# Recommender network on one core: eight features looked up by matmuls, comparisons shared by VectorE and GpSimd, products written from ScalarE's queue

## What is computed

```
e = emb_tables[jnp.arange(F)[None, :], x]            # B=1024, F=32, D=64, V=1000
gram = jnp.einsum('bid,bjd->bij', e, e)
iu, ju = jnp.triu_indices(F, k=1)
cross = gram[:, iu, ju]
h = jnp.concatenate([e.reshape(B, F * D), cross], axis=1)
h = jax.nn.relu(h @ W1 + b1)                          # H1=1024
h = jax.nn.relu(h @ W2 + b2)                          # H2=512
logits = h @ W3 + b3                                  # OUT=1000
return jax.nn.sigmoid(logits)
```

## Time and profile before

| what | value |
|---|---|
| three timed runs | 657.92, 658.48 (median), 665.98 us |
| profiled execution, first to last instruction | 660.4 us, on core 0 |
| PE busy | 456.6 us (69%) |
| DVE, ACT, POOL busy | 291.9, 246.6, 269.1 us |
| mean granted clock of PE | 0.852 of full |
| moved by DMA | 67.60 MB, mean 102 GB/s |

### The profile page before, as it was taken

How to read it: one execution, slowest core, us unless ns; L and a number is a source line. 1 busy time by engine, 2 the same in 40 slices (tenths; PEclk the granted TensorE clock), 3 DMA queues, 4 the chain that set the end, 5 groups by cost and what they waited for, 6 DMA issues and landing times.

```text
span 660.4 us, 8819 instructions
## 1 busy us (share of the span) xinstructions
PE 456.6 (69%) x3344; PEld 434.9 (66%) x3344; DVE 291.9 (44%) x461; ACT 246.6 (37%) x449; POOL 269.1 (41%) x265
## 2 busy tenths in 40 slices
PE   0222137572759876676799899811799999999786
PEld 0012127471749876576699889811799899999786
DVE  6210024150324553253546658610546688846641
ACT  3110023130334342152534666500434776834532
POOL 6777717577540377767100378777000000000000
PEclk9997558585769888768699999955799999999989
DMA  6611101131316211332086424411175305186522
GB/s 195 217 51 26 26 6 23 21 95 52 99 33 251 75 25 22 88 102 71 15 288 187 126 58 116 120 26 26 76 262 177 104 23 164 66 279 188 161 90 63
DMA packets 29145, 67.60 MB, mean 102 GB/s; under 512 B 6418, under 2 KB 12722, under 8 KB 28594
## 3 DMA queue, kind: packets, MB, share of 16 engines
q1 hardware_dynamic: 16834, 54.54, 25.7%
q0 software_dynamic: 8192, 8.40, 6.2%
q10 hardware_dynamic: 4080, 4.10, 2.1%
HBM read 56.63 MB, written 10.39 MB: 101 GB/s over the span
## 4 chain that ended last, share of the span: by engine, by line
PE 51%; another core or an unknown queue 17%; issue 11%; DVE 6%; POOL 5%; ACT 5%; DMA 4%; SPq 0%; ACTq 0%
PE h1p L491 11%; PE h1p L493 10%; PE h1p L492 10%; PE misc L524 8%; POOL emb L255 5%; PE misc L491 3%; PE misc L492 3%; PE misc L493 3%; DVE dg L418 2%; PE misc L513 2%; DVE h1p L435 2%; DMA out_dram<-res 2%; ACT whi L299 1%; ACT z L304 1%
## 5 line engine op out<-in xcount | busy, mean ns | idle before, releaser
L255 POOL DMA_INDIRECT emb<-tables_dram,idx x256 | 267.4, 1045 | 184.9 <-PE misc L513 101.7
L491 PE MATMUL h1p<-xhi,whi 128*128 128x256 f32 x512 | 156.4, 306 | 16.8 <-issue 12.7
L493 PE MATMUL h1p<-xhi,wlo 128*128 128x256 f32 x512 | 151.2, 295 | 12.5 <-issue 12.2
L492 PE MATMUL h1p<-xlo,whi 128*128 128x256 f32 x512 | 151.2, 295 | 8.7 <-issue 8.6
L524 PE MATMUL misc<-z 128*128 128x128 f32 x512 | 78.8, 322 | 89.5 <-ACT dg L315 50.3
L524 PEld LDWEIGHTS misc<-z 128*128 128x128 f32 x512 | 74.2, 233 | 93.7 <-ACT dg L315 51.6
L400 DVE TENSOR_TENSOR wlo<-wraw,whi 128x1024 fp32r<-128x1024 f32 (+1 forms) x80 | 97.2, 1215 | 60.7 <-ACT whi L299 60.2
L491 PEld LDWEIGHTS h1p<-xhi,whi 128*128 128x128 f32 x512 | 104.3, 204 | 18.2 <-issue 13.8
L492 PEld LDWEIGHTS h1p<-xlo,whi 128*128 128x128 f32 x512 | 104.1, 203 | 13.9 <-issue 13.6
L493 PEld LDWEIGHTS h1p<-xhi,wlo 128*128 128x128 f32 x512 | 103.8, 203 | 12.6 <-issue 12.2
L299 ACT CAST whi<-wraw 128x1024 fp32r<-128x1024 f32 (+1 forms) x80 | 84.1, 1052 | 57.6 <-PE h1p L493 34.4
(11 more groups left out here) (39 smaller groups left out, 589.1 us busy)
## 6 DMA issues: line engine op xcount, KB each, us to landing
wraw<-w_dram SPq DMA_DIRECT2D x64, 512.0 KB
wraw<-w_dram SPq DMA_DIRECT2D x16, 500.0 KB
wres<-w_dram SPq DMA_DIRECT2D x8, 512.0 KB, 3.6
emb<-tables_dram,idx POOLq DMA_INDIRECT x256
gram_scratch<-dg SPq DMA_DIRECT2D x4, 1024.0 KB, 3.9
out_dram<-res ACTq DMA_DIRECT2D x16, 250.0 KB
gram_scratch<-dg SPq DMA_DIRECT2D x4, 512.0 KB, 4.8
gc<-gram_scratch SPq DMA_DIRECT2D x16, 128.0 KB, 2.8
```

The lines of the kernel that those rows point to most:

```text
L255: nc.gpsimd.indirect_dma_start(emb[:, k, t, f * D:(f + 1) * D], None, tables, bass.IndirectOffsetOnAxis(ap=idx[:, t, 2 * k + f:2 * k + f + ...
L491: nc.tensor.matmul(dst, whi[:, slot, cols], hi, start=start, stop=False, skip_group_check=True)
L492: nc.tensor.matmul(dst, whi[:, slot, cols], lo, start=False, stop=False, skip_group_check=True)
L493: return nc.tensor.matmul(dst, wlo[:, slot, cols], hi, start=False, stop=stop, skip_group_check=True)
```

## The change

- Features 24 to 31 (pairs 12 to 15, `LOOKS`) are no longer gathered. For each pair and block a new step "look" loads the two tables in full as 125 partitions by 8 entries (`VP`, `VC`), splits them like weights into hi and lo side by side, and PE multiplies them with eight 0/1 matrices of 125x256 for each feature: entry [p, c, sample] is 1 where the id is 8p + c. These come from comparisons of the ids (loaded to all partitions by `load_x`) with a constant. Of the eight comparisons of a half-step, DVE makes c < 6 (first block) or c < 5, GpSimd the others, placed between its gathers by `gathers_before`. Three of these matrices' buffers are there (`HOTS`). PE makes 16 matmuls of 125x128 by 256 columns in a look.
- Features 0 to 23 are gathered: 48 gathers a block, in the order of pairs, for both tiles together, into two buffers of `emb`; the wait for the transposes of two blocks before stands from block 2 on. PE transposes two pairs at a time (`tr`), and ACT and DVE then take 128x512 (hi, lo) and two times 64x256 (`z`) in one go.
- Layer 1 follows the tiles as they come, from the first block on (`schedule`), with layers 2 and 3 of the block before between; everything is written out, without hardware loops. No weights stay resident: every step is loaded, six steps ahead.
- `z` uses 64 partitions for each tile, and the products are 128 matmuls of 64x64 with 64 rows each for a block, in 4 groups; ACT and DVE each take two parts of 32x512 from each group.
- `dg` is written to DRAM once (1 MB, without the second copy of 0.5 MB), from ACT's queue, and read back by four DMAs from ACT's queue (`move`); the outputs are issued by SP, after a wait for the sigmoid.
- b1 is a row of the pair weights against a row of ones. ACT applies relu out of PSUM for both hidden layers; the separate passes of DVE (L435) are gone.
- `weight_lo` subtracts in four quarters of 128x256 where it was one instruction of 128x1024.

```diff
+VP, VC = 125, 8
+HOTS = 3
+LEAD = 24
 QB = NB // 4
-GJ = QB // 4
+GROUPS = QB // 16
 CROSS = 4
...
+def schedule():
...
+    yield ("look", 0, 12)
+    for n in range(BLOCKS):
+        yield ("tr", n, 0)
+        yield from emb(n, 12, 0)
+        yield ("look", n, 13)
+        yield from emb(n, 1)
+        yield from l2(n - 1, 0)
+        yield ("tr", n, 1)
+        yield from emb(n, 13)
+        yield from l2(n - 1, 1)
+        yield ("tr", n, 2)
+        yield from emb(n, 2)
+        yield from l2(n - 1, 2)
+        yield ("look", n, 14)
+        yield from emb(n, 3)
+        yield from l2(n - 1, 3)
+        yield ("tr", n, 3)
+        yield from emb(n, 14)
+        yield from l3(n - 1, 0)
+        yield ("look", n, 15)
+        yield from emb(n, 4)
+        yield ("tr", n, 4)
+        yield from l3(n - 1, 1)
+        yield ("tr", n, 5)
+        yield from emb(n, 15, 5)
+        yield ("gram", n)
+        yield from emb(n, 6, 7, 8)
+        yield ("move", n)
+        yield from l3(n - 1, 2)
+        yield from emb(n, 9)
+        yield from l3(n - 1, 3)
+        yield from emb(n, 10)
+        yield ("pairs", n)
+        yield from emb(n, 11)
+        for k in range(CROSS):
+            yield ("pair", n, k)
+        yield ("h1", n)
+        if n + 1 < BLOCKS:
+            yield ("look", n + 1, 12)
+    for k in range(4):
+        yield from l2(BLOCKS - 1, k)
+    for k in range(4):
+        yield from l3(BLOCKS - 1, k)
...
+def first_on_gpsimd(h):
+    return 6 if h < 2 * LOOKS else 5
...
+def gathers_before(h, c):
+    n, at = divmod(h, 2 * LOOKS)
+    ready = (0, 0, 6, 10, 18, 24, 28, 32)[at] if n == 0 else 4 * GT * n + LEAD - 10 + 6 * at
+    return min(BLOCKS * 4 * GT, max(0, ready - 2 * (VC - 1 - c)))
...
+            def load_x(i):
+                if i >= len(LOOKED):
+                    return
+                _, n, k = LOOKED[i]
+                if i >= 2:
+                    sp.wait_ge(s_hotv, 2 * (i - 1))
+                    sp.wait_ge(s_hotp, 2 * (i - 1))
+                src = bass.AP(tensor=xt.tensor, offset=2 * k * B + n * NB, ap=[[0, VP], [B, 2], [1, NB]])
+                sp.dma_start(xb[0:VP, i % 2, :, :], src).then_inc(s_xb[i % 2], 16)
...
+            for kind, n, *k in ITEMS:
+                if (kind, n, *k) in STEP:
+                    load(STEP[kind, n, k[0]] + LOADS_AHEAD)
+                if kind == "look":
+                    load_x(LOOK[kind, n, k[0]] + 2)
+                if kind == "out":
+                    j = k[0]
+                    sp.wait_ge(s_sig, 4 * n + j + 1)
+                    sp.dma_start(out.rearrange("(s p) b -> p s b", p=OT)[:, 2 * j:2 * j + 2, n * NB:(n + 1) * NB],
+                                 res[:, j % 2, :].rearrange("p (s b) -> p s b", s=2)).then_inc(s_out[j % 2], 16)
...
+            def compare(h, c):
+                i, f = divmod(h, 2)
+                if c == first_on_gpsimd(h):
+                    pool.wait_ge(s_xb[i % 2], 16 * (i // 2 + 1))
+                    if h >= HOTS:
+                        pool.wait_ge(s_used, used_after(*LOOKED[(h - HOTS) // 2]))
+                last = nc.gpsimd.tensor_scalar(hot[0:VP, h % HOTS, c, :], xb[0:VP, i % 2, f, :],
+                                               vals[0:VP, c:c + 1], None, ALU.is_equal)
+                if c == VC - 1:
+                    last.then_inc(s_hotp, 1)
+            comparisons = [(h, c) for h in range(2 * len(LOOKED)) for c in range(first_on_gpsimd(h), VC)]
+            gathers = [(n, k, t, f) for n in range(BLOCKS) for k in range(GT) for t in range(BT) for f in range(2)]
+            made = 0
+            for g, (n, k, t, f) in enumerate(gathers):
+                while made < len(comparisons) and gathers_before(*comparisons[made]) <= g:
+                    compare(*comparisons[made])
+                    made += 1
+                m = k // 2
+                if g == 0:
+                    pool.wait_ge(s_idx, 1)
+                if (n, k, t, f) == (1, 0, 0, 0):
+                    pool.wait_ge(s_idx, 2)
+                if n >= 2 and (k % 2, t, f) == (0, 0, 0):
+                    pool.wait_ge(s_t, GP * (n - 2) + m + 1)
+                nc.gpsimd.indirect_dma_start(
+                    emb[:, n % 2, k, t, f * D:(f + 1) * D], None, tables,
+                    bass.IndirectOffsetOnAxis(ap=idx[:, BT * n + t, 2 * k + f:2 * k + f + 1], axis=0),
+                ).then_inc(s_emb[n % 2][m], 16)
+            for h, c in comparisons[made:]:
+                compare(h, c)
...
+            def looked_up_hi(n, k):
+                act.wait_ge(s_used, used_after("look", n, k))
+                read = bank_of("look", n, k)
+                for f in range(2):
+                    nc.scalar.copy(xhi[D * f:D * (f + 1), k, :], read[0:D, f, :])
+                nc.scalar.copy(xlo[0:D, k, :], read[D:P, 0, :]).then_inc(s_zeven, 1)
+            def gram_copies(n):
+                for g in range(GROUPS):
+                    act.wait_ge(s_gram, GROUPS * n + g + 1)
+                    for c in range(2):
+                        last = nc.scalar.copy(dg_of(g, c), gram_diagonal(g, c))
                     last.then_inc(s_dga, 1)
+                if n > 0:
+                    act.wait_ge(s_gc, 64 * n)
+                act.wait_ge(s_dga, GROUPS * (n + 1))
+                act.wait_ge(s_dgv, GROUPS * (n + 1))
+                act.dma_start(gd, dg[:]).then_inc(s_gdw, 16)
+            def move(n):
+                act.wait_ge(s_gdw, 16 * (n + 1))
+                if n > 0:
+                    act.wait_ge(s_gclo, n)
+                else:
+                    act.wait_ge(s_gcones, 1)
+                for kk in range(4):
+                    src = bass.AP(tensor=gd.tensor, offset=(CROSS * kk + 1) * QB,
+                                  ap=[[(F + 1) * QB, F - 1], [F * F * QB, 4], [1, CROSS * QB]])
+                    act.dma_start(gc[F * kk:F * (kk + 1) - 1, :, :, :].rearrange("i c s q -> i c (s q)"),
+                                  src).then_inc(s_gc, 16)
...
+            def weight_lo(u):
+                if u >= len(STEPS):
                     return
+                w = width(STEPS[u][0])
+                dve.wait_ge(s_whi, u + 1)
+                for i in range(4):
+                    part = slice(w // 4 * i, w // 4 * (i + 1))
+                    if STEPS[u][0] == "look":
+                        part = slice(VC // 2 * i, VC // 2 * (i + 1))
+                        last = nc.vector.tensor_tensor(table_part(u % RING, 1)[:, part, :], table_raw(u)[:, part, :],
+                                                       table_part(u % RING, 0)[:, part, :].bitcast(fp32), ALU.subtract)
+                    else:
+                        last = nc.vector.tensor_tensor(wlo(u % RING)[:, part], wraw[:, u % RAWS, part],
+                                                       whi(u % RING)[:, part].bitcast(fp32), ALU.subtract)
+                last.then_inc(s_wlo, 1)
...
+            def compare(i):
+                if i >= len(LOOKED):
+                    return
+                dve.wait_ge(s_xb[i % 2], 16 * (i // 2 + 1))
+                for f in range(2):
+                    h = 2 * i + f
+                    if h >= HOTS:
+                        dve.wait_ge(s_used, used_after(*LOOKED[(h - HOTS) // 2]))
+                    for c in range(first_on_gpsimd(h)):
+                        last = nc.vector.tensor_scalar(hot[0:VP, h % HOTS, c, :], xb[0:VP, i % 2, f, :],
+                                                       vals[0:VP, c:c + 1], None, ALU.is_equal)
+                    last.then_inc(s_hotv, 1)
...
+            def look_up(n, k, slot):
+                i, a = SLOT["look", n, k], LOOK["look", n, k]
+                slot_free(i, n)
+                for f in range(2):
+                    pe.wait_ge(s_hotv, 2 * a + f + 1)
+                    for c in range(VC):
+                        if c == first_on_gpsimd(2 * a + f):
+                            pe.wait_ge(s_hotp, 2 * a + f + 1)
+                        last = nc.tensor.matmul(misc[:, i % 2, NB * f:NB * (f + 1)],
+                                                wsplit[0:VP, slot, P * (VC * f + c):P * (VC * f + c + 1)],
+                                                hot[0:VP, (2 * a + f) % HOTS, c, :], start=(f, c) == (0, 0),
+                                                stop=c == VC - 1, skip_group_check=True)
+                return last
+            def gram(n):
+                pe.wait_ge(s_zeven, SLOTS * (n + 1))
+                pe.wait_ge(s_zodd, SLOTS * (n + 1))
+                if n > 0:
+                    pe.wait_ge(s_sig, outs_before(("gram", n)))
+                for g in range(GROUPS):
+                    if g >= 2:
+                        pe.wait_ge(s_dga, GROUPS * n + g - 1)
+                        pe.wait_ge(s_dgv, GROUPS * n + g - 1)
+                    for q in range(8):
+                        for h in range(2):
+                            for t in range(BT):
```

(4 more changed lines are left out.)

697 lines of the change are left out of this document (321 added, 376 removed).

## The result

The changed kernel takes 634.82 us (median of 4 runs, 632.97 to 637.81). The kernel before, run beside it, takes 662.23 (657.92 to 669.17); the ratio is 0.9597, 95% interval [0.9526, 0.9667]. The forecast was 546 us, in a range of 498 to 632. The sign is right, the time lies outside the range.

A forecast was written before the change was run, and what follows sets the result against it. Before: PE bounds only block 3, and stalls beside dense gathers cost the others. After: PE and DVE together bound the blocks; 142 + 123 + 123 + 118 and a tail of 40 give 546 us, range 498 to 632.

The forecast's parts named there:

- The sign: Whole kernel: faster than before by more than 2% (below 645 us), given a chance of 0.91.
- the write and the read back: Products through DRAM in each block: about 13 us, hidden behind six steps (17 us); up to 10 us if uncovered.
- Block 0's stall: Block 0, gathers 32 to 58 without comparison: a stall mostly covered by the gathers, 2 us added, block 142 us.
- The stalls of blocks 1 and 2: Blocks 1 and 2, beside gathers: comparisons act as pauses, leaving 5 us of stall in each, from 36 and 46.
- Rival B: Blocks 1 to 3: stalls stay because GpSimd's comparisons are no pause for the code; about 626 us, chance 0.18.
- the missing code: Stalls beside gathers: engine code is not delivered while POOL gathers densely, but arrives in a pause of a microsecond.
- Products: PE's 256 product matmuls in each block: 20 us taken, between 7 (side by side in the array) and 28.6.
- A block's DVE: VectorE's work in each of blocks 1 to 3: 105 us, with 1.70 us for a step's four quarter subtractions.
- GpSimd's comparison: One 256-element comparison on POOL between gathers: 0.8 us taken, within 0.3 to 1.3.
- Rival C: Blocks 1 to 3: VectorE is the bound, stopped by GpSimd's comparisons, 136 us a block; about 603 us, chance 0.12.
- Rival D: POOL sets the pace because its comparisons are dear; slower than before from 3.7 us a comparison, chance 0.04.
- Rival E: Looks wait for late 0/1 matrices, so layer 1 does not follow the tiles; 7 us each gives 658, chance 0.04.

The follow-up runs named there:

- e1: Changed kernel with each 31-row read back of the products cut into reads of 16 and 15 rows: 498.14 us, 0.9964 of before.
- f1: Changed kernel run again without edit, in a set where the kernel before took 498.0 us: 597.86 us, 1.1986 of before.
- e2: Changed kernel with the write and the four 31-row reads of the products issued from SyncE's queue instead of ScalarE's: 575.98 us, 1.1536 of before.
- e3: Kernel before the change, with each 32-row read of the products cut into one of 31 rows and one of 1: 572.06 us, 1.1457 of before.
- first set: The first comparison runs, both kernels without edit: changed kernel 634.8 us, kernel before 662.2 us.
- h2: Kernel before with an unused GpSimd comparison after every second gather and POOL's loop written out, beside before at 664.74 us: 602.36 us, 0.908.
- h1: Changed kernel with reads of 16 and 15 rows, all comparisons on VectorE and whole subtractions, beside before at 664.74 us: 626.37 us, 0.9433.
- f2: Kernel before the change, run again without edit for a trace: 498.24 us.
- k2: The kernel of h1 without further edit, run where before takes 498.64 us: 483.19 us, 0.9686 of before.
- g2: e1 with all comparisons on VectorE and none on GpSimd: 493.08 us, 0.9872 of before.
- g1: e1 with each weight subtraction of VectorE again one instruction of 128x1024 instead of four quarters: 510.69 us, 1.0228 of before.

## Why the prediction was wrong

**The step that failed** is the one on the write and the read back: "four reads, two casts of a microsecond each: about 13 us, hidden. If the cover went, up to 10 us a block would show." It took the four reads to be like those of before. They are not: the diff changes the first dimension of the access from F = 32 rows to F - 1 = 31. One read of 31 rows costs a median of 5.2 us to issue where one of 32 had 0.43, and 35 us pass from the first issue to the cast of the products, where e1 needs 13. It showed 26, 21, 28 and 22 us in four blocks (f1 against e1), 97 us where at most 40 were allowed. e1, e2 and e3 hold it from three sides: spread the rows and the wait goes; move the queue and only 22 us go; put the shape into before and 72 us come.

The Trainium skill (DMA: Bandwidth & Descriptors, "How many engines (k)") says that a DMA is spread over the largest number of engines, up to 16, that divides the slowest dimension of both its sides, and gives 127 partitions as an example that lands on one. By that rule 31 rows run on one engine, 32 and 16 on sixteen, 15 on fifteen. The trace agrees: the read keeps 6.0% of sixteen engines busy. The prediction did not apply the rule; by it the hiding would have been in doubt from the diff alone. The sum also has no term for the clock that PE loses by waiting (16 us of busy time, f1 against e1).

**Block 0's stall** was "mostly covered by the gathers" and priced at 2 us. In the first set it cost about 23: block 0 takes 185 us there and 162 in f1. Up to 86 us PE has made 276 matmuls in both; from 86 to 117 it makes 71 here and 440 in f1. Stretches of the kernel after, 86 to 117 us, then its first DMA queue, 90 to 115, which answer to the earlier trace rows:

```profile
86.00:117.00 31.00, 14.57 (x71) 11.84 (x71) 5.59 (x14) 4.39 (x8) 25.47 (x27) 0.55 0.16 39
```

```profile
q0 software_dynamic: 563, 0.57, 11.5%
```

The 26 gathers without a comparison, named in the prediction, go out from 64.8 to 97.6 us, and the stall begins within them. So the place was found rightly; but a stall beside gathers is not covered by them when steps of layer 1 wait there too. In its timeline (88 to 104 us) PE idles 1.0 to 2.5 us ahead of most instructions, put down to issue. And the stall did not end as the prediction had it. From 97.6 us on a comparison stands after every second gather, and PE, with 2, 6, 8 and 20 matmuls in 5 us each, needs some 13 us to come back to work without gaps:

```profile
95.00:100.00 5.00, 0.75 (x2) 0.86 (x3) 0.00 (x0) 0.00 (x0) 3.96 (x5) 0.50 0.11 20
100.00:105.00 5.00, 2.13 (x6) 1.29 (x5) 0.00 (x0) 0.00 (x0) 4.39 (x5) 0.50 0.09 20
105.00:110.00 5.00, 2.42 (x8) 1.74 (x7) 0.00 (x0) 0.00 (x0) 4.31 (x5) 0.50 0.10 20
```

One pause of a microsecond is thus not enough to end a stall that has begun.

**The stalls of blocks 1 and 2** (5 us left) went as forecast: between the first set and f1 these blocks differ by 6 us each, where before lost 31 and 43. Some stall can hide behind the wait for the reads in both runs, so 6 us is what shows, not all that there was. Rival B, whose 626 us lie nearest to the result, is refuted as a mechanism by that and by h2; that its number came close is chance. Of the reading "code for the engines is not delivered while POOL issues gathers densely, and is delivered in a pause of a microsecond" two parts held in the slow sets: the stalls come with dense gathers (h1), and regular pauses take them away (h2). Its middle, the missing code, is not shown: packets came by the number of matmuls made, stall or not (119, 128 and 131). And f2 has the same gathers at the same pace without the stalls. What decides between the two was not found; it is not in the kernel, since before and f2, the kernel after and f1, and h1 and k2 are each one program.

**PE's and DVE's terms.** Durations of the kernel after by form, which answer to the earlier trace rows:

```profile
L492 DVE TENSOR_TENSOR wsplit<-wraw,wsplit 128x256 fp32r<-128x256 f32 x384 | 142.0, 436 | 87.0 <-ACT wsplit L374 85.1 <-issue 1.0
...
L332 POOL TENSOR_SCALAR hot<-xb,vals 125x256 fp32r<-125x256 int32 x88 | 93.3, 1061 | 175.3 <-PE misc L628 167.3 <-DMA xb<-xt_dram 5.4
L564 DVE TENSOR_SCALAR hot<-xb,vals 125x256 fp32r<-125x256 int32 x168 | 59.7, 427 | 2.9 <-DMA xb<-xt_dram 2.5
...
L647 PE MATMUL misc<-z 64*64 64x64 f32 x1024 | 33.7, 262 | 12.3 <-issue 11.0 <-DVE dg L520 0.8
...
L520 DVE COPY dg<-misc 32x512 f32<-32x512 f32 x32 | 22.2, 693 | 23.2 <-PE misc L647 19.0 <-remote 4.0
L501 DVE COPY z<-misc 64x256 f32<-64x256 f32 x48 | 20.5, 428 | 1.1
```

- Products: 20 us a block taken, between 7 and 28.6. They take 5.6 to 7.3 us in e1's four blocks, waits for the copies included, and in block 1 the first 128 instructions run without a break:

```profile
208.63 2.27 PE L648 MATMUL misc<-z 64*64 64x64 f32 x128
211.87 0.94 PE L648 MATMUL misc<-z 64*64 64x64 f32 x49 [0.96 <-DVE dg L521]
214.16 1.64 PE L648 MATMUL misc<-z 64*64 64x64 f32 x79 [1.36 <-issue]
```

2.27 us for 128 is 0.018 each, a sixth of the 0.112 that the 128x128 ones took. The low end, "if products in different quarters of the array ran side by side, 7", was the right one; it was set aside because no row showed overlap. That they ran side by side is a reading of this price; no run changes the placement alone. This term was 13 us too dear in each block.
- A block's DVE: 105 us forecast, 91, 91 and 87 measured in e1. One quarter at 436 ns and one comparison at 427 were as priced, but in a row they overlap: 384 quarters are 142.0 us of busy time in this list, 0.37 each, so a step costs 1.5 us and not 1.70, some 7 us less in a block. The z copies (428 ns, priced at 620) and the copies of products (693, priced at 900) were too dear as well.
- GpSimd's comparison: 0.8 us taken, 1.06 measured, inside 0.3 to 1.3.
- Blocks of e1: 136, 115, 110, 108 and a tail of 31, against 142, 123, 123, 118 and 40. Apart from the read the terms were dear by 48 us in all; on PE's side the products are the largest part.

**Rival C** (DVE bound, held up by GpSimd) is refuted: DVE is busy 87 to 91 us of e1's later blocks, not 136, and the delay is mostly in the other direction. DVE's quarter gains 19 ns from the absence of GpSimd's comparisons (g2), while GpSimd's comparison loses 152 ns to longer subtractions (g1). The Trainium skill (SBUF — State Buffer, two separate sides) gives the port pair to whichever instruction starts first and has the other blocked fully; in the mean of these traces DVE is hardly slowed. **Rival D** is refuted by its price, 1.06 us against the 3.7 it needs. Its sign came true all the same in f1, by another mechanism: 1.20 of before where before has no stalls. **Rival E** is refuted: PE waited for GpSimd's comparisons twice in the kernel after, 7.7 us in all.

**Where the forecast gain went** has two answers. In the first set: 546, less 48 for terms that were too dear (e1 against the forecast), plus 100 for the reads (f1 against e1), plus 37 for what that set costs (first set against f1), is 635. This sum is a chain of differences of measured times and so must close; it says where the time went only as far as each difference has one cause. Where before takes 498 us there was nothing of the kind to gain. In blocks 1 to 3 PE is busy 289 us in f2 (91, 99, 99) and 299 in e1, since the looks put back what the cheaper products save and the clock is a little lower, and the blocks last 309 and 333. The change takes gathers off POOL, and in these blocks POOL was not the bound. The shorter tail, 31 us for 49, gives most of the difference back.

Left open: what slows the engines beside gathers in some sets (no two sets are known to be of one chip, so chip and moment can't be told apart); and e1 where before takes 662. An estimate from 498 and the 37 us that the changed kernel lost in that set is 535 us; it was not run.

## What to carry to other kernels

When a diff changes the number of rows of a DMA, price the DMA again: 31 rows in place of 32 turned reads that landed in 2.9 us into 24 and held the issuing queue for 16, and a second issue of half a microsecond, with 16 and 15 rows, undid it. A gain that comes from a stall is worth only what the stall costs where the kernel will run; time the old kernel on several chips before pricing its cure. Before a missing packet is called the cause of a stall, count the instructions between packets: here they came by the instruction, at any speed. Cutting up work so that another engine gets its turn (quarters, shared comparisons) pays when the other engine is on the path: quarters gained 12 us with GpSimd's comparisons and cost 10 without them, and those comparisons cost 5 us in e1 where before takes 500, but block 0 took 185 us with them and 249 without (h1) where before takes 662 to 665.

## What the runs showed of the hardware

- A read of 31 rows of 4 x 1 KB: 5.2 us of queue each (at most 9.5), four landing after 24 us at 6.0% of sixteen engines; the same bytes as 16 and 15 rows: 0.46 us of queue each, and 2.6 us of PE's waits in four blocks.
- The same program at 498 and 662 us, or at 483 and 626: in the slow case PE made 46 matmuls in 110 us, one each 2.8 us in the stretch shown, beside GpSimd gathers every 1.25 us; a GpSimd operation of 1.08 to 1.12 us after every second gather made the two cases equal, at 602.
- Instruction packets (q8) of the kernel before came once in 119, 128 and 131 matmuls, in 15, 54 and 15.5 us.
- After an idle time of 10.44 us PE's clock was 0.50: 21 matmuls in 4 us, where 253 took 30 us at 1.00.
- GpSimd's comparison (125x256, 1061 to 1098 ns) grew to 1250 beside 128x1024 subtractions on DVE, while DVE's quarter was 438 ns beside GpSimd's comparisons and 419 without them.
- DVE subtractions of 128x256, 436 ns each, took 0.37 us of busy time each in a row; one of 128x1024 took 1.22.
- 128 matmuls of 64x64 by 64 columns on two row and two column halves of the array ran in 2.27 us, 0.018 each.
